# Loading a score stack in two pieces: the first group of heads apart from the other three, the key high parts on GpSimd's queue

## The reference, cut to what matters

```python
# x: (4, 512, 128), 16 heads of 8, rank-32 adapters, 8 experts, top 2
def lora_linear(x, w, b, la, lb):
    return x @ w.T + b + 0.5 * (x @ la.T @ lb.T)
qkv = lora_linear(x, w_attn, b_attn, la_attn, lb_attn)
q, k, v = split(qkv)                       # each to (B, H, T, 8)
att = softmax(where(causal, q @ k.T / sqrt(8), -inf))
x = layernorm(x + lora_linear(att @ v, w_proj, b_proj, la_proj, lb_proj))
probs = softmax(x @ router_w)
weights, idx = top_k(probs, 2)             # weights divided by their sum
x = layernorm(x + sum over the two experts of
              weights * ((silu(x @ gate[e]) * (x @ up[e])) @ down[e]))
```

## Time and profile before

| | |
|---|---|
| runs | 295.1, 295.37, 296.13 us (median 295.37) |
| the profiled execution | 294.57 us, its span 292.8 us |
| mean granted clock of TensorE | 0.964 |
| PE matmul busy | 244.6 us (84%) |
| VectorE busy | 218.4 us (75%) |
| ScalarE busy | 160.8 us (55%) |
| GpSimd busy | 171.2 us (58%) |
| hardware DMA queue of SyncE (q1) | 28016 packets, 18.15 MB |

### The profile page before, as it was taken

One profiled execution on the slowest core, in us unless ns is written; L12 is line 12 of the kernel. 1 busy time (PEld: TensorE's weight loads), 2 busy tenths in 40 slices (PEclk: granted clock), 3 DMA queues, 4 the chain that ended last, 5 costly groups with the idle time before them and its releaser, 6 DMA issues.

```text
span 292.8 us, 7079 instructions
## 1 busy us (share of the span) xinstructions
PE 244.6 (84%) x2286; PEld 142.9 (49%) x2286; DVE 218.4 (75%) x572; ACT 160.8 (55%) x276; POOL 171.2 (58%) x307
## 2 busy tenths in 40 slices
PE   4978768988999799898898989989989999999200
PEld 3454422332444334343343437777767778877100
DVE  6377999999898988989789965668945555554960
ACT  3644567666777677875769693523323333333170
POOL 7708836566453776738768653785655555433750
PEclk9989999999999999999999999999999999999755
DMA  6399013344021032320320032113433331035052
GB/s 166 79 219 201 10 41 92 97 111 109 4 75 55 27 102 87 97 76 22 104 86 22 23 73 75 45 40 101 143 101 90 100 93 36 30 109 133 4 143 72
DMA packets 32835, 24.09 MB, mean 82 GB/s; under 512 B 5652, under 2 KB 31735, under 8 KB 32776
## 3 DMA queue, kind: packets, MB, share of 16 engines
q1 hardware_dynamic: 28016, 18.15, 23.9%
q0 software_dynamic: 2624, 4.47, 5.0%
q10 hardware_dynamic: 2160, 1.02, 1.4%
HBM read 10.56 MB, written 6.80 MB: 59 GB/s over the span
## 4 chain that ended last, share of the span: by engine, by line
PE 46%; DVE 22%; issue 9%; SPq 7%; DMA 7%; ACT 4%; POOL 3%; POOLq 0%; DVEq 0%; ACTq 0%
DVE negm L1012 12%; PE slot L1682 11%; PE pvo L1436 6%; PE pvo L1698 6%; PE slot L1418 4%; PE slot L1690 3%; PE slot L1398 3%; PE slot L1391 2%; SPq L361 2%; ACT Pt L875 2%; DMA Ks<-early 2%; PE misc L1444 1%; SPq L439 1%; POOL rows_scratch L616 1%; DMA Ks<-chosen_scratch 1%
## 5 line engine op out<-in xcount | busy, mean ns | idle before, releaser
L1012 DVE TENSOR_REDUCE negm<-slot 128x2 f32<-128x1024 f32 (+2 forms) x96 | 96.1, 1042 | 13.5 <-PE slot L1398 12.9
L875 ACT ACTIVATE Pt<-slot 128x1024 f32<-128x1024 f32 (+1 forms) x96 | 80.7, 881 | 28.9 <-PE slot L1418 28.9
L718 POOL DMA_INDIRECT chosen_scratch<-Ks,Qs x39 | 38.4, 984 | 33.9 <-ACT Ks L926 27.4
L590 POOL TENSOR_SCALAR_AFFINE_SELECT Pt<-Pt 128x512 f32<-128x512 f32 x56 | 35.7, 648 | 34.4 <-ACT Pt L875 34.3
L1682 PE MATMUL slot<-GUW,Pt 128*128 x156 | 52.8, 461 | 0.0
L1436 PE MATMUL pvo<-Pt,V 128*9 128x128 f32 (+3 forms) x512 | 46.3, 435 | 1.8 <-POOL Pt L590 1.8
L616 POOL DMA_INDIRECT rows_scratch<-rows,place x32 | 32.0, 999 | 19.3 <-issue 5.1
L1243 DVE COPY Pt<-slot 128x256 f32<-128x256 f32 x39 | 16.6, 425 | 33.1 <-PE slot L1690 32.2
L926 ACT ACTIVATE Ks<-pvo,Qs 128x128 f32<-128x128 f32 x39 | 14.3, 367 | 44.5 <-PE pvo L1698 44.5
L1418 PE MATMUL slot<-Qs,Ks 64*128 64x512 bf16 (+3 forms) x256 | 31.4, 301 | 7.7 <-DVE negm L1012 7.7
L1698 PE MATMUL pvo<-DW,Pt 128*128 (+1 forms) x234 | 32.6, 275 | 0.7 <-ACT Ks L926 0.7
(11 more groups left out here) (229 smaller groups left out, 367.5 us busy)
## 6 DMA issues: line engine op xcount, KB each, us to landing
Qs<-rows_scratch SPq DMA_DIRECT2D x39, 65.0 KB, 2.0
Qs<-early SPq DMA_DIRECT2D x12, 128.0 KB, 3.7
Qs<-DW SPq DMA_DIRECT2D x12, 128.0 KB, 2.4
Ks<-DW SPq DMA_DIRECT2D x12, 128.0 KB, 2.4
GUW<-in_L_ffn_gate_proj_dram SPq DMA_DIRECT2D x8, 176.0 KB, 2.4
GUW<-in_L_ffn_up_proj_dram SPq DMA_DIRECT2D x8, 176.0 KB, 2.5
Ks<-early SPq DMA_DIRECT2D x9, 128.0 KB, 3.3
rows_scratch<-fill SPq DMA_DIRECT2D x8, 130.0 KB
```

What stands on the lines that cost most here:

```text
L590: pool.affine_select(out=v, in_=v, compare_op=ALU.is_ge, fill=0.0, base=0, pattern=[[0, HQ], [1, P]], channel_multiplier=-1).then_inc(sele ...
L718: pool.indirect_dma_start(chosen_scratch, bass.IndirectOffsetOnAxis(xg[:, j, C:C + 1].bitcast(U32), 0), ys[:, j, :], None, bounds_check=2 ...
L875: act.activation(p_view(g % 2, kb)[:, h0:h0 + heads, :].rearrange("p (c a) q -> p a c q", a=2), t_view(u, k_slot(g, u)), ACT.Exp, scale=SC ...
L1012: dve.tensor_reduce(negm[:, g % 2, :, h0 // 2:(h0 + heads) // 2, qb], s_view(u, q_slot(g, u)), AX_X, ALU.max, negate=True).then_inc(max_do ...
```

## The change

It does five things.

1. A stack DMA is split in two pieces, `PIECES`: group 0 of the batch (32 rows of parts, 32 KB) and groups 1 to 3 (96 rows, 96 KB). `STACK_DMAS` goes from 12 to 24. This holds for all four batches. The columns of `WT` and the bias `bqk` are permuted piece by piece to match: four small copies for two, four small DMAs for two.
2. For batch 0 SyncE issues the pieces of group 0 first, as their parts come out, counted on `first_loaded`; then the other pieces, on `stacks_loaded[0]`. TensorE waits for the first before unit 0 and for the rest before unit 6.
3. The key high parts of batch 0 are issued by GpSimd (both pieces, `keys_loaded`) instead of ScalarE.
4. On SyncE `store_maxrows(0)` moves between `load_parts(1, 0)` and `load_parts(1, 1)`. On VectorE the copy of `WPT` moves behind the splits of batch 1.
5. On TensorE the projections of batch 2 move from ahead of unit 0 to between units 1, 2 and 3, the values of batch 2 and the transposes of batch 3 to behind units 3 and 4.

```diff
-        STACK_DMAS = 2 * PRODUCTS
-        def stack_rows(eng, b, s, part):
+        STACK_DMAS = 4 * PRODUCTS
+        KEYS_HIGH = sum(part == 0 for part in K_PARTS)
+        PIECES = ((0, 1), (1, QPB))
+
+        def stack_rows(eng, b, s, part, piece, loaded):
+            g0, g1 = PIECES[piece]
             for e in range(PRODUCTS):
                 if (Q_PARTS, K_PARTS)[s][e] == part:
-                    eng.dma_start((Qs, Ks)[s][e:P:BLOCK, QPB * b:QPB * (b + 1)].rearrange("p g c t -> p (g c t)"),
-                                  parts[b][:, s, part, :]).then_inc(stacks_loaded[b], 16)
+                    eng.dma_start((Qs, Ks)[s][e:P:BLOCK, QPB * b + g0:QPB * b + g1].rearrange("p g c t -> p (g c t)"),
+                                  parts[b][HQ * D * g0:HQ * D * g1, s, part, :]).then_inc(loaded, 16)
+        def wait_first_group(eng):
+            eng.wait_ge(first_loaded, 16 * (2 * PRODUCTS - KEYS_HIGH))
+            eng.wait_ge(keys_loaded[0], 16 * KEYS_HIGH)
+
+        def wait_other_groups(eng):
+            eng.wait_ge(stacks_loaded[0], 16 * (2 * PRODUCTS - KEYS_HIGH))
+            eng.wait_ge(keys_loaded[1], 16 * KEYS_HIGH)
...
             def load_parts(b, s):
                 sp.wait_ge(cleared[b], 1)
-                sp.wait_ge(high_out[s], b + 1)
-                stack_rows(sp, b, s, 0)
...
+                for part, out_ in enumerate((high_out, mid_out, low_out)):
+                    sp.wait_ge(out_[s], b + 1)
+                    for piece in range(2):
+                        stack_rows(sp, b, s, part, piece, stacks_loaded[b])
...
-            load_parts(0, 0)
-            sp.wait_ge(low_out[1], 1)
-            stack_rows(sp, 0, 1, 1)
-            stack_rows(sp, 0, 1, 2)
+            sp.wait_ge(cleared[0], 1)
+            for part, out_ in enumerate((high_out, mid_out, low_out)):
+                sp.wait_ge(out_[0], 1)
+                stack_rows(sp, 0, 0, part, 0, first_loaded)
+            for part, out_ in enumerate((mid_out, low_out)):
+                sp.wait_ge(out_[1], 1)
+                stack_rows(sp, 0, 1, 1 + part, 0, first_loaded)
+            for part in range(PARTS):
+                stack_rows(sp, 0, 0, part, 1, stacks_loaded[0])
+            for part in range(1, PARTS):
+                stack_rows(sp, 0, 1, part, 1, stacks_loaded[0])
             load_parts(1, 0)
+            store_maxrows(0)
             load_parts(1, 1)
-            store_maxrows(0)
             store_maxrows(1)
...
+            pool.wait_ge(high_out[1], 1)
+            for piece in range(2):
+                stack_rows(pool, 0, 1, 0, piece, keys_loaded[piece])
             load_ones(1)
...
             for s in range(2):
-                act.dma_start(bqk[:, s:s + 1], b_attn[s * C:(s + 1) * C].rearrange("(g a d) -> a d g", a=2, d=D),
-                              allow_slow_non_contiguous=True).then_inc(bqk_loaded, 16)
+                for g0, g1 in PIECES:
+                    n0, n1 = HQ * D * g0, HQ * D * g1
+                    act.dma_start(bqk[n0:n1, s:s + 1], b_attn[s * C + n0:s * C + n1].rearrange("(g a d) -> a d g", a=2, d=D),
+                                  allow_slow_non_contiguous=True).then_inc(bqk_loaded, 16)
...
-            act.wait_ge(cleared[0], 1)
-            act.wait_ge(high_out[1], 1)
-            stack_rows(act, 0, 1, 0)
             copy_high(1, 0, slot[2][:, 0:T])
...
-                dve.tensor_copy(WT[:, j, :].rearrange("p (a d g) -> p a d g", a=2, d=D),
-                                slot[2][:, j * C:(j + 1) * C].rearrange("p (g a d) -> p a d g", a=2, d=D))
+                for g0, g1 in PIECES:
+                    n0, n1 = HQ * D * g0, HQ * D * g1
+                    dve.tensor_copy(WT[:, j, n0:n1].rearrange("p (a d g) -> p a d g", a=2, d=D),
+                                    slot[2][:, j * C + n0:j * C + n1].rearrange("p (g a d) -> p a d g", a=2, d=D))
...
-            pe.wait_ge(weights_out, 3)
-            pe.wait_ge(xT_out, 3)
-            project_qk(2, 0, pvo[:, :])
-            project_qk(2, 1, misc[:, :])
-            pe.wait_ge(stacks_loaded[0], 16 * STACK_DMAS)
+            wait_first_group(pe)
             pe.wait_ge(ones_loaded[0], 32)
...
+                    if n == NU:
+                        wait_other_groups(pe)
                     scores_q(g, u)
 
                     if n == 1:
+                        pe.wait_ge(weights_out, 3)
+                        pe.wait_ge(xT_out, 3)
+                        project_qk(2, 0, pvo[:, :])
+                    if n == 2:
+                        project_qk(2, 1, misc[:, :])
+                    if n == 3:
                         pe.wait_ge(qk_out, 1)
                         project_values(2, pvo[:, :])
+                    if n == 4:
                         pe.wait_ge(qk_out, 2)
                         transpose_x(3)
```

More of the change, by code:

```diff
@@ L287, in causal_attention_then_top2_experts @@
         stacks_loaded = [sem(f"stacks_loaded{b}") for b in range(B)]
+        first_loaded, keys_loaded = sem("first_loaded"), [sem(f"keys_loaded{i}") for i in range(2)]
         cleared = [sem(f"cleared{b}") for b in range(B)]
@@ L391, in load_parts @@
                 sp.wait_ge(cleared[b], 1)
-                sp.wait_ge(high_out[s], b + 1)
-                stack_rows(sp, b, s, 0)
-                sp.wait_ge(mid_out[s], b + 1)
-                stack_rows(sp, b, s, 1)
-                sp.wait_ge(low_out[s], b + 1)
-                stack_rows(sp, b, s, 2)
+                for part, out_ in enumerate((high_out, mid_out, low_out)):
+                    sp.wait_ge(out_[s], b + 1)
+                    for piece in range(2):
+                        stack_rows(sp, b, s, part, piece, stacks_loaded[b])
             def store_maxrows(g):
@@ L814, in _ @@
             copy_xT(1)
-            act.wait_ge(bqk_loaded, 32)
+            act.wait_ge(bqk_loaded, 64)
             copy_high(0, 0, slot[0][:, 0:T])
             copy_high(0, 1, slot[0][:, T:2 * T])
-            act.wait_ge(cleared[0], 1)
-            act.wait_ge(high_out[1], 1)
-            stack_rows(act, 0, 1, 0)
             copy_high(1, 0, slot[2][:, 0:T])
@@ L1001, in _ @@
                     split(b, s, rest[:, s, :])
-                if b == 0:
-                    dve.wait_ge(weights_full, 3)
-                    dve.tensor_copy(WPT[:, :], pvo[:, 0:C]).then_inc(weights_out, 1)
+            dve.wait_ge(weights_full, 3)
+            dve.tensor_copy(WPT[:, :], pvo[:, 0:C]).then_inc(weights_out, 1)
             def row_max(g, u):
@@ L1215, in _ @@
             step(0)
-            for b in range(2):
-                dve.wait_ge(stacks_loaded[b], 16 * STACK_DMAS)
+            wait_first_group(dve)
+            wait_other_groups(dve)
+            dve.wait_ge(stacks_loaded[1], 16 * STACK_DMAS)
             for g in range(1, 4):
```

## The result

The changed kernel took 302.91, 300.91, 303.61 and 302.81 us, median 302.86 us. The kernel before, run beside it four times, had a median of 295.38 us. The ratio is 1.024, with a 95% interval of 1.019 to 1.029: slower by 7.5 us. The forecast was 300.2 us, slower.

A forecast was written before the change was run, and what follows sets the result against it. SyncE's issue queue, with slack before, would become the bound: 0 (start) + 3.8 (queue) + 1.0 (long issues) = +4.8 us, from 294.57 to 299.4 us, 300.2 us as median. Range 293.8 to 303.5 us, about 0.8.

The forecast's parts named there:

- Start 0.3 us later: Ahead of the parts: extra weight copies and bias DMAs move the first stack DMA from 12.49 to 12.8 us.
- The first group at 20.9 us: SyncE's nine group 0 pieces end at 18.6 us and land 2.3 us later, 2.4 us earlier than now.
- TensorE's 8.0 us for units 0 to 6, so a term of 0: TensorE before step 0: the moved projections use up the 2.4 us gained; batch 3's second projection stays near 31.4 us.
- Up to 2.3 us would come back: Start of the scores: what would be regained if batch 2's moved projections were free again.
- The slot of a piece, 0.64 us: SyncE's queue: each piece takes a whole's issue slot; 90 pieces and six pairs make step 5 3.8 us late.
- The rival of keeping up: SyncE's slots are below 0.597 us and the kernel is faster, nearly all within 293.2 to 294.4 us; chance 0.22.
- issues that are hidden anyway: Rival on SyncE's queue: slots of 0.56 to 0.60 us, no long issues, time unchanged at 294.6 to 296.2 us; chance 0.14.
- Long issues, 1.0 us: SyncE's queue: unusually long issues now lie on the path and add 1.0 us, ends 0 and 4.9 us.
- Landing of the maxima, 2.0 us: End of SyncE's queue: group 5's maxima, issued by 80.2 us, land 2.0 us later, at 82.2 us.
- slots of 0.60 to 0.68 us with 0 to 3 us of long issues: The likeliest case, SyncE's queue too slow: 297 to 304 us, likeliest 300.2 us, chance 0.58.
- Step by step: Lateness of the maxima: about 0.1 us for group 0, 0.6 us for group 1, then 0.7 us more for each.
- VectorE's wait for batch 1: Batch 1's stack issues end at 41.3 us, land at 43.6 us, before VectorE's step 0 ends at 43.8 us: no cost.

The follow-up runs named there:

- c1: The kernel before, unchanged, run again on the chip of most follow-up runs: 303.3 us (one execution).
- e10: The kernel before with only the changed kernel's move of batch 2's projections, values and transposes: 297.97 us against 294.95 us for the kernel before, ratio 1.013.
- e2: The changed kernel, all pieces kept, with batch 2's projections ahead of unit 0 again: 314.35 us against 305.09 us for the kernel before, ratio 1.037.
- e4: The changed kernel with pieces for batch 0 only and batch 2's projections ahead of unit 0: 303.69 us against 305.09 us before, ratio 1.002.
- e5: The kernel before plus a 256-byte DMA behind each of the 36 stack DMAs of batches 1 to 3: 313.01 us against 303.05 us, ratio 1.037.
- e1: The changed kernel with pieces for batch 0 only, batches 1 to 3 whole: 306.02 us against 305.09 us for the kernel before, ratio 1.009.
- e3: The changed kernel with batch 1 whole, pieces for batches 0, 2 and 3: 308.89 us against 305.09 us for the kernel before, ratio 1.019.
- e7: e4 with the values of batch 3 one unit earlier: 302.42 us against 303.05 us for the kernel before, ratio 1.000.
- e11: The kernel of e7 once more, on another chip: 302.75 us against 303.37 us for the kernel before, ratio 1.000.

## Why the prediction was right, and which terms were off

The direction, the mechanism and the place were right. The result, 302.9 us, lies in the range, 0.6 us under its upper end of 303.5 us, and the likeliest value, 300.2 us, was 2.7 us too low. Point by point:

**Start 0.3 us later.** SyncE's first stack DMA went out at 12.63 us against 12.49 us, 0.1 us. One execution can't show so little: with the same code up to there, the kernel before had this DMA at 12.30 us in c1, and e10 at 11.34 us.

**The first group at 20.9 us.** Its nine pieces were issued from 12.63 to 18.39 us, and unit 0 started at 20.98 us. The first maximum began at 21.79 us, forecast near 21.5. That this held was luck in part. The profile counts a landing from the start of an issue, and the prediction added its 2.3 us to the end of the last one (18.6 us). The last piece of SyncE was issued from 17.80 us and landed 3.0 us later: read rightly, the sum would have come out 0.6 us earlier, and the landing was longer than the least by about as much. In the same way the 4.40 us of the earlier trace rows are the time to landing of the issue that started at 18.88 us (the last three took SyncE 1.89 us from 17.59 us), not a wait for the one at 18.23 us.

**TensorE's 8.0 us for units 0 to 6, so a term of 0.** The projection of batch 3 behind unit 6 started at 28.94 us, 7.96 us after unit 0; the second one at 31.39 us, forecast 31.4. The first moved projection took 1.97 us at a granted clock of 0.50, the second 1.12 us. So the term held, and the moved projections take the time as said. e10 shows their cost by itself, 1.7 us of step 0. But they are not the whole reason. In the changed kernel the full queue holds step 0 as well (0.31 us in its timeline), and e2, with the projections back, gains nothing. The prediction had only 0.1 us for that wait and nothing on this. "Up to 2.3 us would come back" was too much: e4, with the projections back and a free queue, has step 0 0.8 us earlier than before, and no time.

**The slot of a piece, 0.64 us.** Nine took 5.8 us (12.63 to 18.43), and twelve without a long one 7.62 us (45.56 to 53.18), so 0.635 us. The pair with its gaps took 1.64 us. Both held. The rival of keeping up would have needed 0.597 us; the other, issues that are hidden anyway, falls with e5. The Trainium skill ("DMA: Bandwidth & Descriptors", "Issuing engines are not separate DMA queues") has the time to initiate a DMA as usually small relative to the DMA. Here it is 0.594 us out of 2.3 us from issue to landing, but what decides is 90 of them in a row on one sequencer, and the measured 8.4 us stand against the 0 that the prediction drew from that sentence.

**Long issues, 1.0 us: this is the term that failed.** The forecast had the maxima of group 5 issued at 80.2 us; the changed kernel ended them at 85.84 us. Among the issues from 18.43 us on nine last over 0.8 us; what they take above 0.60 us (0.72 us in a pair) adds up to 5.6 us, the longest 1.94, 1.60, 1.57 and 1.19 us. With 0.2 us less for the earlier start, 80.2 - 0.2 + 5.6 = 85.6 us, within 0.2 us of what was measured. The prediction's argument that long issues would be rarer, since transfers are less dense, was wrong: 5.6 us over 93 issues is the share of before (2.4 us over 45) and a little more. Even its upper end, 4.9 us by the share of before, was 0.7 us too low. The last section has what the longest of them go with.

**Landing of the maxima, 2.0 us.** The 65 KB of the earlier trace rows were a good neighbour for 6 KB: the chain has 1.82 us for the second of a pair, from 85.10 us. But both count from the start of the issue, and the prediction added the 2.0 us to its end. The issue ended at 85.84 us and the matmul behind it started at 86.97 us, 1.13 us later. The same at 45.45 and 46.58 us. So the term was 0.9 us too much, by a misreading of the row.

**The sum.** 0 + 3.8 + 1.0 was forecast for step 5; it came as 3.8 - 0.2 + 5.6 - 0.9 = 8.3 us, measured 8.6 us. Errors of opposite sign leave the forecast 3.8 us short at step 5. The spans differ by 8.4 us (301.2 less 292.8 us), the medians by 7.5 us.

**The bounds.** The prediction gives "slots of 0.60 to 0.68 us with 0 to 3 us of long issues" as 297 to 304 us. Its own sum gives 295.7 to 305.9 us for these ends, and it has no reason for the narrower ones. Slots of 0.64 us with 5.6 us of long issues, as measured, are outside the case that it called likeliest, though the time is inside its 297 to 304 us. Two terms that came out smaller keep it there: the landing, and the 0.8 us put between the profiled execution and the median, which the changed kernel does not show (302.91 and 302.86 us).

**Step by step.** Group 1 was to be 0.6 us late and was 2.2 us late: by then six long issues with 2.7 us had gone by. From there 0.7 us a step was forecast, and 0.7, 1.6, 1.6 and 2.5 us came: a step without a long issue among its twelve pieces loses what was worked out, the others 1 us more and above; the last also since step 5 began 8.07 us behind step 4 before, not 8.62 us.

**VectorE's wait for batch 1.** The issues of batch 1 ended at 43.88 us instead of 41.3 us. VectorE's next maximum was released by GpSimd's work on the maxima at 45.87 us, after 1.43 us of idle time. The maxima's own wait hides any cost of this one, and no run tells them apart.

**That it is the queue** rests on three runs: e1 takes the extra issues away and the growing loss goes with them; e2 leaves them and moves the projections, and it stays; e5 adds them to the kernel before with almost nothing to carry, and it comes. e3 shows that the slack is used up first.

## What to carry to other kernels

On SyncE an issue of these stack DMAs cost the same from 256 bytes to 128 KB (594 to 599 ns), so a list of DMAs is costed by its number of issues against the length of the loop that feeds from it: 12 x 0.64 + 1.64 us against 8.62 us was already enough to decide here. Cut a transfer only where its early part is waited for (the first batch), and keep the rest whole; here even that brought no time (ratios 1.002 in e4, 1.000 in e7 and e11). Work moved off the time in which an engine waits is not free where it goes (1.7 us of step 0 in e10), and a pause that is left behind can cost the clock as well (0.50 behind the 5.83 us there), so read the granted clock behind each pause before counting on an earlier start.

## What the hardware showed beyond that

**Long issues come with instruction packets.** In the changed kernel five packets of 16 KB on the instruction queue q8 fall between 12 and 87 us, at 26, 41, 55, 69 and 81 us; the issues of 1.06, 1.60, 1.19, 1.57 and 1.94 us start at 27.18, 41.65, 56.49, 69.54 and 81.69 us. In e5 the packets are at 24, 45, 57, 70 and 82 us, and issues of 0.94, 1.50, 1.83, 1.26 and 1.44 us start at 24.59, 45.93, 57.46, 70.35 and 82.27 us. In e11 one falls at 22 us, with the first of the three issues that took 2.97 us. The window of the changed kernel from 41 to 44 us:

```profile
q8 instruction: 1, 0.02, 3.0%
```

These packets don't follow SyncE's list. The kernel before has them too, at 25, 41, 53, 64 and 75 us. From the first matmul of `scores_k` in steps 2, 3 and 4 they come 0.8, 3.1 and 5.5 us later before, 0.0, 3.2 and 5.3 us later in the changed kernel and 0.6, 3.4 and 5.3 us later in e5, though SyncE issues twelve DMAs with each pair of maxima there and six before. So it is not shown that SyncE's sequencer waits for its own instructions, nor that more issues bring more packets. What differs is what they meet: before, the two at 25 and 41 us came with issues of 1.01 and 1.43 us, the one at 53 us and the one at 75 us fell into SyncE's idle time, and beside the one at 64 us a pair of maxima took its usual 1.54 us. In the changed kernel SyncE is never idle, and each of the five has a long issue beside it; together these make 4.4 of the 5.6 us. How a packet lengthens an issue, if it does, no run shows. Some long issues (0.96 us at 18.43 us) have no such packet beside them.

**GpSimd issues pieces of the same form faster**, 527 ns against 594 ns of SyncE (medians of six and of the 24 of `Qs<-early`).

**The same program starts differently from one execution to the next.** Step 0 was at 34.0 and at 36.23 us in e7 and e11. One long issue and the low clock behind the longer pause go with the difference. Differences of this size at the start of one profiled execution are not evidence on their own.
